# Widening in a convolution and frequency-filter kernel as four float16 products instead of one float32 product

## The reference

```python
x = x + conv3x3(group_norm(x), binary_weight)            # layer 0, sign(w) * alpha
h = einsum('oc,bchw->bohw', w_in, group_norm(x))         # layer 1: 64 -> 256 channels ("widening")
f = rfft2(8x8 patches of h) * fft_filt ; h = irfft2(f)   # a filter per channel and frequency
h = depthwise conv3x3(h, w_dw)
x1, x2 = split(h) ; x = x + einsum('oc,bchw->bohw', w_out, gelu(x1) * x2)
```

## Time and profile before

| | |
|---|---|
| median of three runs | 5607.01 us |
| the profiled execution | 5608.77 us |
| its span (first to last instruction) | 5606.9 us |
| granted TensorE clock, mean | 0.997 of 2.4 GHz |
| TensorE (PE) busy | 5467.3 us, 98% |
| TensorE weight loads (PEld) | 3466.9 us, 62% |
| VectorE (DVE) | 4848.7 us, 86% |
| ScalarE (ACT) | 3314.4 us, 59% |
| GpSimd (POOL) | 3779.9 us, 67% |
| DMA | mean 39 GB/s |

### The profile page before, as it was taken

The page is one execution under the profiler, slowest core; times in us unless marked ns, Lnnn a source line. Parts: engine busy times, 40 slices in busy tenths (PEclk is TensorE's granted clock), DMA queues, the critical chain, the costliest instruction groups (busy, mean ns, idle before and its releaser), DMA issues.

```text
span 5606.9 us, 159317 instructions
## 1 busy us (share of the span) xinstructions
PE 5467.3 (98%) x69156; PEld 3466.9 (62%) x69156; DVE 4848.7 (86%) x6149; ACT 3314.4 (59%) x4194; POOL 3779.9 (67%) x2055
## 2 busy tenths in 40 slices
PE   5999999999999999999999999999999999999998
PEld 4666666666666666666666666666666666666665
DVE  6889888898888989888898888988889888898887
ACT  3656656566565665656656565565655656566565
POOL 3767666676666766666666676666666767676666
PEclk9999999999999999999999999999999999999999
DMA  2011010110101101011010100101011010110000
GB/s 99 18 48 41 35 41 28 51 38 35 51 21 48 38 35 54 18 51 38 35 51 20 55 31 35 54 35 41 31 38 48 35 41 31 48 41 18 22 21 28
DMA packets 43783, 216.61 MB, mean 39 GB/s; under 512 B 5366, under 2 KB 6104, under 8 KB 36952
## 3 DMA queue, kind: packets, MB, share of 16 engines
q1 hardware_dynamic: 43096, 206.42, 9.6%
HBM read 103.64 MB, written 102.76 MB: 37 GB/s over the span
## 4 chain that ended last, share of the span: by engine, by line
PE 78%; DVE 17%; issue 4%; ACT 1%; DMA 0%; DVEq 0%; POOL 0%; SPq 0%; ACTq 0%; POOLq 0%
PE PS L895 19%; PE PS L912 18%; PE PS L857 14%; PE PS L885 14%; DVE v L632 8%; PE PS L925 7%; PE PS L875 4%; DVE g L655 3%; PE PS L866 2%; DVE hf L625 2%; DVE bn L563 1%; DVE PS L648 1%; ACT carry L464 1%; DVE nbx L580 0%; DVE Xa L662 0%
## 5 line engine op out<-in xcount | busy, mean ns | idle before, releaser
L346 POOL TENSOR_TENSOR v_lo<-v,v_hi 128x1024 f16<-128x1024 f32 (+1 forms) x1792 | 3356.8, 1895 | 1712.1 <-ACT v_hi L443 1701.6
L632 DVE TENSOR_TENSOR v<-PS,smul 128x1024 f32<-128x1024 f32 (+1 forms) x1792 | 1903.5, 1084 | 313.4 <-PE PS L895 288.6
L443 ACT ACTIVATE v_hi<-v 128x1024 f16<-128x1024 f32 (+1 forms) x1792 | 1652.5, 945 | 788.8 <-DVE v L632 583.3
L895 PE MATMUL PS<-hf,c_nodes 64*128 64x512 f32 (+1 forms) x7168 | 1724.0, 573 | 55.8 <-DVE v L632 35.5
L912 PEld LDWEIGHTS PS<-c_ext,v_hi 128*128 128x128 f16 x14336 | 1130.4, 97 | 458.1 <-issue 249.5
L912 PE MATMUL PS<-c_ext,v_hi 128*128 128x100 f16 (+2 forms) x14336 | 1257.8, 203 | 20.2 <-ACT carry L464 16.1
L912 PE MATMUL PS<-c_ext,v_lo 128*128 128x100 f16 (+2 forms) x14336 | 1249.8, 202 | 0.0
L912 PEld LDWEIGHTS PS<-c_ext,v_lo 128*128 128x128 f16 x14336 | 1117.9, 97 | 1.4
L625 DVE TENSOR_TENSOR hf<-PS,mult 128x1024 f32<-128x1024 f32 (+1 forms) x896 | 962.9, 1086 | 148.0 <-PE PS L885 134.4
L895 PEld LDWEIGHTS PS<-hf,c_nodes 64*128 64x128 f32 x7168 | 577.0, 185 | 634.6 <-DVE v L632 313.7
L885 PE MATMUL PS<-win_sb,xf 64*128 64x256 f32 x6272 | 850.1, 399 | 4.1 <-ACT xf L432 1.0
(11 more groups left out here) (63 smaller groups left out, 3801.7 us busy)
## 6 DMA issues: line engine op xcount, KB each, us to landing
out_x<-Xa SPq DMA_DIRECT2D x96, 448.0 KB, 2.5
out_x<-Xb SPq DMA_DIRECT2D x96, 448.0 KB, 2.5
Xa<-in_x SPq DMA_DIRECT2D x8, 2240.0 KB, 7.9
Xb<-in_x SPq DMA_DIRECT2D x8, 2240.0 KB, 8.0
Xa<-in_x SPq DMA_DIRECT2D x8, 1792.0 KB, 6.7
Xb<-in_x SPq DMA_DIRECT2D x8, 1792.0 KB, 6.9
Xa<-in_x SPq DMA_DIRECT2D x8, 1344.0 KB, 5.8
Xb<-in_x SPq DMA_DIRECT2D x8, 1344.0 KB, 6.4
```

What stands on the lines that cost most here:

```text
L346: nc.gpsimd.tensor_tensor(v_lo[:, img, :, k0:k1, :], v32[:, V_BUF[kind(b, s)][img][grp], :, 0:k1 - k0, :], v_hi[:, img, :, k0:k1, :], ALU. ...
L443: nc.scalar.activation(v_hi[:, img, :, k0:k1, :], v32[:, V_BUF[kind(b, s)][img][grp], :, 0:k1 - k0, :], ACT.Copy).then_inc(act_vhi[img], 1)
L632: nc.vector.tensor_tensor(v32[:, V_BUF[kind(b, s)][img][grp], :, 0:k1 - k0, :], PS[:, bank:bank + 2, 0:(k1 - k0) * C2].rearrange("p i (k c ...
L895: last = nc.tensor.matmul(PS[:, bank + side, 0:(k1 - k0) * C2], c_nodes[half, :], hf[half, img, k0:k1, :].rearrange("p k c -> p (k c)"), s ...
```

## The change

`w_in` and the spectrum are each held as two float16 parts, high (the rounded value) and low (the rest, rounded), and widening makes four float16 products that accumulate in PSUM: high x high, low x high, high x low, low x low. `win_hi` and `win_lo` are made once by VectorE. The spectrum's high part is made by a second ScalarE pass over `xf` (`spectrum_high`), the low part by GpSimd (`spectrum_low`). `xf` now shares the memory of `xT`, so `pixels` waits for the low part of the strip before. Widening waits for `pool_xl`. Besides, the orders of groups (`HF_ORDER`, `V_ORDER`, `V_BUF`) and the order of instructions of every engine in both kinds of step are new; all waits and banks follow them. Nothing else is changed.

The new order on TensorE: in a conv step projection 0, interpolation (image 0, half 0), widening of groups 3, 2, 0, projection 1, evaluation (0, 2), widening 1, interpolation (0, 1), evaluations (0, 3), (0, 1), (0, 0), then the convolutions and the rest as before. Before it was projection 0, widening 2, 0, interpolation (0, 0), widening 3, 1, evaluation (0, 3), interpolation (0, 1), evaluations (0, 2), (0, 1), projection 1, evaluation (0, 0). In a plain step it is projection 0, interpolation (0, 0), widening 0, 2, interpolation (0, 1), widening 1, evaluation (0, 0), projection 1, widening 3, transposes, evaluations (0, 2), (0, 3), interpolation (1, 0), evaluations (0, 1), (1, 1), interpolation (1, 1), forward transform, evaluations (1, 2), (1, 0), (1, 3). Before it was projection 0, interpolation (0, 0), widening 3, 0, 2, projection 1, widening 1, evaluation (0, 0), interpolation (0, 1), evaluation (0, 2), transposes, interpolation (1, 0), evaluations (0, 3), (0, 1), (1, 1), then the same.

On VectorE filters and weightings follow the same orders; the first carry addition goes ahead of the filters, in a conv step the second residual ahead of weighting (0, 0) and the gate of image 0 behind it, in a plain step the statistics of x are spread anew and the second residual comes behind the gate of image 1. The rest of the diff's core:

```diff
-    HF_ORDER = {"plain": (3, 0, 2, 1), "conv": (2, 0, 3, 1)}
-    V_ORDER = {"plain": ((0, 2, 3, 1), (1, 2, 0, 3)), "conv": ((3, 2, 1, 0), (3, 2, 0, 1))}
+    HF_ORDER = {"plain": (0, 2, 1, 3), "conv": (3, 2, 0, 1)}
+    V_ORDER = {"plain": ((0, 2, 3, 1), (1, 2, 0, 3)), "conv": ((2, 3, 1, 0), (3, 2, 0, 1))}
     V_BUF = {"plain": [{0: 0, 2: 1, 3: 2, 1: 0}, {1: 1, 2: 2, 0: 0, 3: 1}],
- "conv": [{3: 0, 2: 1, 1: 2, 0: 0}, {3: 1, 2: 2, 0: 0, 1: 1}]}
+ "conv": [{2: 0, 3: 1, 1: 2, 0: 0}, {3: 1, 2: 2, 0: 0, 1: 1}]}
...
+        xf = xT
+        xf_hi = sb("xf_hi", [128, NBLK, BPX], F16)
+        xf_lo = sb("xf_lo", [128, NBLK, BPX], F16)
...
+def spectrum_low(n, s):
+    pool.wait_ge(act_xh, n * STRIPS + s + 1)
+    nc.gpsimd.tensor_tensor(xf_lo[:], xf[:], xf_hi[:], ALU.subtract).then_inc(pool_xl, 1)
...
@@ GpSimd, conv and plain order
+            if mid:
+                low_nodes(mid[0], mid[1], 0, 2)
             if more and len(NORM_STEPS.get(t, ())) > 1:
                 low_strip(n + 1, NORM_STEPS[t][1])
             if mid:
                 low_nodes(mid[0], mid[1], 0, 3)
-                low_nodes(mid[0], mid[1], 0, 2)
                 low_nodes(mid[0], mid[1], 0, 1)
                 low_nodes(mid[0], mid[1], 0, 0)
                 low_nodes(mid[0], mid[1], 1, 3)
+            if front:
+                spectrum_low(n, t)
+            if mid:
                 low_nodes(mid[0], mid[1], 1, 2)
                 low_nodes(mid[0], mid[1], 1, 0)
                 low_nodes(mid[0], mid[1], 1, 1)
@@ -375,11 +389,14 @@
                 low_nodes(mid[0], mid[1], 0, 3)
                 low_nodes(mid[0], mid[1], 0, 1)
                 low_nodes(mid[0], mid[1], 1, 1)
+            if front:
+                spectrum_low(n, t)
+            if mid:
                 low_nodes(mid[0], mid[1], 1, 2)
+                low_nodes(mid[0], mid[1], 1, 0)
             if more and len(NORM_STEPS.get(t, ())) > 0:
                 low_strip(n + 1, NORM_STEPS[t][0])
             if mid:
-                low_nodes(mid[0], mid[1], 1, 0)
                 low_nodes(mid[0], mid[1], 1, 3)
...
 def pixels(n, s, bank):
     act.wait_ge(pe_xT, n * STRIPS + s + 1)
+    if n or s:
+        act.wait_ge(pool_xl, n * STRIPS + s)
     nc.scalar.activation(xT[:].rearrange("p k c -> p (k c)"), flat(bank, NBLK * 128), ACT.Copy).then_inc(act_xT, 1)
 def spectrum(n, s, bank):
-    act.wait_ge(pe_xf, n * STRIPS + s + 1)
+    i = n * STRIPS + s
+    act.wait_ge(pe_xf, i + 1)
     nc.scalar.activation(xf[:].rearrange("p k (s f) -> p s k f", f=P * P),
                          PS[:, bank:bank + 2, 0:NBLK * P * P].rearrange("p s (k f) -> p s k f", f=P * P),
                          ACT.Copy).then_inc(act_xf, 1)
+
+def spectrum_high(n, s):
+    i = n * STRIPS + s
+    act.wait_ge(act_xf, i + 1)
+    if i:
+        act.wait_ge(pe_hf, 4 * i)
+    nc.scalar.activation(xf_hi[:], xf[:], ACT.Copy).then_inc(act_xh, 1)
...
@@ ScalarE, conv and plain order
         if more and CONV_FROM <= t <= CONV_TO:
             if up:
                 gelu(up[0], up[1], 0)
+            if more and len(NORM_STEPS.get(t, ())) > 0:
+                strip32(n + 1, 1 - par, NORM_STEPS[t][0], False)
+            if up:
                 keep0(up[0], up[1], 0)
             if more and len(NORM_STEPS.get(t, ())) > 0:
-                strip32(n + 1, 1 - par, NORM_STEPS[t][0], False)
                 strip16(n + 1, 1 - par, NORM_STEPS[t][0], False)
             if more and len(NORM_STEPS.get(t, ())) > 1:
                 strip32(n + 1, 1 - par, NORM_STEPS[t][1], False)
+            if mid:
+                high_nodes(mid[0], mid[1], 0, 2)
+            if more and len(NORM_STEPS.get(t, ())) > 1:
                 strip16(n + 1, 1 - par, NORM_STEPS[t][1], False)
             if mid:
                 high_nodes(mid[0], mid[1], 0, 3)
-                high_nodes(mid[0], mid[1], 0, 2)
             if up:
                 keep1(up[0], up[1], 0)
+            if mid:
+                high_nodes(mid[0], mid[1], 0, 1)
             if front:
                 pixels(n, t, BANK_Q)
-            if mid:
-                high_nodes(mid[0], mid[1], 0, 1)
-                high_nodes(mid[0], mid[1], 0, 0)
+                normalise_patches(n, par, t + 1, True)
             if up:
                 gelu(up[0], up[1], 1)
                 keep0(up[0], up[1], 1)
+            if mid:
+                high_nodes(mid[0], mid[1], 0, 0)
             if front:
                 spectrum(n, t, BANK_P)
+                spectrum_high(n, t)
             if mid:
                 high_nodes(mid[0], mid[1], 1, 3)
             if up:
                 keep1(up[0], up[1], 1)
-            if front:
-                normalise_patches(n, par, t + 1, True)
             if mid:
                 high_nodes(mid[0], mid[1], 1, 2)
                 high_nodes(mid[0], mid[1], 1, 0)
@@ -508,10 +540,10 @@
                 keep0(up[0], up[1], 0)
             if mid:
                 high_nodes(mid[0], mid[1], 0, 0)
-            if up:
-                keep1(up[0], up[1], 0)
             if front:
                 pixels(n, t, BANK_P)
+            if up:
+                keep1(up[0], up[1], 0)
             if mid:
                 high_nodes(mid[0], mid[1], 0, 2)
             if up:
@@ -525,18 +557,18 @@
                 spectrum(n, t, BANK_P)
             if up:
                 keep1(up[0], up[1], 1)
-            if mid:
-                high_nodes(mid[0], mid[1], 1, 2)
-            if more and len(NORM_STEPS.get(t, ())) > 0:
-                strip32(n + 1, 1 - par, NORM_STEPS[t][0], False)
-                strip16(n + 1, 1 - par, NORM_STEPS[t][0], False)
-            if mid:
-                high_nodes(mid[0], mid[1], 1, 0)
             if front:
+                spectrum_high(n, t)
                 if t < STRIPS - 1:
                     normalise_patches(n, par, t + 1, True)
                 elif more:
                     normalise_patches(n + 1, 1 - par, 0, True)
+            if mid:
+                high_nodes(mid[0], mid[1], 1, 2)
+                high_nodes(mid[0], mid[1], 1, 0)
+            if more and len(NORM_STEPS.get(t, ())) > 0:
+                strip32(n + 1, 1 - par, NORM_STEPS[t][0], False)
+                strip16(n + 1, 1 - par, NORM_STEPS[t][0], False)
             if mid:
                 high_nodes(mid[0], mid[1], 1, 3)
...
@@ VectorE, prologue
+nc.vector.tensor_copy(win_hi[:], win_sb).then_inc(dve_prep, 1)
+dve.wait_ge(dve_prep, 3)
+nc.vector.tensor_tensor(win_lo[:], win_sb, win_hi[:], ALU.subtract).then_inc(dve_prep, 1)
...
 def widened(b, s, grp, bank):
     k0, k1 = GROUPS[grp]
-    pe.wait_ge(act_xf, b * STRIPS + s + 1)
+    pe.wait_ge(pool_xl, b * STRIPS + s + 1)
     for k in range(k0, k1):
-        for r in range(IMGS):
-            last = nc.tensor.matmul(PS[:, bank + r, (k - k0) * C2:(k - k0 + 1) * C2], xf[r * C:(r + 1) * C, k, :],
-                                    win_sb[r * C:(r + 1) * C, :], start=True, stop=True)
+        for part, (xf, win) in enumerate(((xf_hi, win_hi), (xf_lo, win_hi), (xf_hi, win_lo), (xf_lo, win_lo))):
+            for r in range(IMGS):
+                last = nc.tensor.matmul(PS[:, bank + r, (k - k0) * C2:(k - k0 + 1) * C2],
+                                        xf[r * C:(r + 1) * C, k, :], win[r * C:(r + 1) * C, :],
+                                        start=part == 0, stop=part == 3)
     last.then_inc(pe_hf, 1)
```

More of the change, by code:

```diff
@@ L701, in image @@
                             weighted(b, s, 0, 1, BANK_Q)
-                        if up:
-                            gated(up[0], up[1], 0)
+                        if done:
+                            residual(done[0], (par + done[2]) % 2, done[1], 1)
                         if mid:
@@ L710, in image @@
                             convolved(n + 1, 1 - par, conv_strips(t)[1], BANK_P)
-                        if done:
-                            residual(done[0], (par + done[2]) % 2, done[1], 1)
                         if up:
@@ L719, in image @@
                             stats_1(n + 1, 1 - par, conv_strips(t)[1])
-                        if more and t == GROUP1_STEP - 1:
-                            channels_1(n + 1)
                         if mid:
@@ L731, in image @@
                             weighted(b, s, 1, 1, BANK_Q)
+                        if more and t == GROUP1_STEP - 1:
+                            channels_1(n + 1)
                     else:
@@ L737, in image @@
                         if mid:
-                            filtered(b, s, 3, BANK_P)
+                            filtered(b, s, 0, BANK_Q)
+                            filtered(b, s, 2, BANK_P)
+                        if more and len(STAT_STEPS.get(t, ())) > 1:
+                            stats_x(n + 1, 1 - par, STAT_STEPS[t][1])
                         if more and t == GROUP1_STEP:
@@ L762, in image @@
                             weighted(b, s, 0, 2, BANK_Q)
-                        if more and len(STAT_STEPS.get(t, ())) > 1:
```

(31 more changed lines are left out.)

122 lines of the change are left out of this document (51 added, 71 removed).

## The result

| | before | after |
|---|---|---|
| median of 4 runs, us | 5607.29 (5606.2 to 5607.81) | 5566.68 (5564.79 to 5567.16) |
| profiled execution, us | 5608.8 | 5564.8 |
| its span, us | 5606.9 | 5563.0 |

The ratio is 0.9927 [0.991, 0.9944]: 40.6 us or 0.73% faster. The forecast was 5509, 98 us faster. The sign is right and the time lies in the range, but less than half of the gain came.

The account below looks back on a forecast made before the run. PE alone was taken to bound convolution steps; in plain steps VectorE was only 1.2 us behind. 105 x 0.48 = 50.4 plus 119 x 0.42 = 50.0 less 0.7 gave 99.7 us: 5608.8 to 5509, range 5450 to 5578.

Parts of the forecast that it names:

- the best stretch, 0.97 us for two blocks, has 0.06 us a block over that: Float32 widening on PE: the best stretch exceeds the 0.427 us streaming of a product pair by 0.06 us a block.
- the convolution step's 0.48: Widening in each of 105 convolution steps: 3.79 to 3.31 us, 0.48 saved, 50.4 us in all.
- about 0.1 us at a group whose bank is released late: PE's widening stretches: the rest of 3.53 and 3.79 us is about 0.1 us at each late-released bank.
- The plain step's 0.42: Each of 119 plain steps: a walk of the new order gave 0.55 us less, minus 0.13 for tighter feed; 50.0 us.
- Rival D: Handoffs between PE and VectorE through the two bank pairs eat everything, so the time stays the same; chance 0.05.
- so all of it counts: Convolution step: it is PE-bound, so the whole 0.48 us saved in widening shortens the step.
- rival A: VectorE, busy 20.09 of 21.27 us, is the wall in plain steps; only convolution steps give, 5558 us; chance 0.12.
- Rival B: The new GpSimd subtraction before widening comes late, from 0.75 us of lateness on a loss; about 5700 us; chance 0.08.
- Rival C: Loads of a row half don't go under its own matmul: 0.204 us a pair, 6080 us; chance 0.05.
- Rival E: The new orders also take out waits that were there: 0.8 us saved a step, 5430 us; chance 0.05.
- The costs of ScalarE and GpSimd: 224 second passes on ScalarE, 0.94 us each, 211 us; 224 subtractions on GpSimd, 1837 ns each, 411 us; both have room.
- The start-up: The prologue: two copies of 128x256 and a wait on VectorE, 0.7 us once.

Follow-up runs that it names:

- e7: Kernel after with VectorE's filtering and weighting over half of the 256 columns, the rest of their outputs zero, PE's work whole; 5408.62 us, 0.9646 to before.
- e9: Kernel before with the new orders, float32 widening and no feed, VectorE's filtering and weighting over half of the columns; 5432.49 us, 0.9689 to before.
- e11: Kernel after with only the product form undone: widening is float32 again, while orders, second ScalarE pass, GpSimd subtraction and waits stay; 5596.32 us, 0.9982 to before.
- e8: Kernel before with VectorE's filtering and weighting over half of the columns, the rest of their outputs zero; 5432.65 us, 0.9689 to before.
- e1: Kernel before with the new orders alone: widening stays one float32 product, no second ScalarE pass, subtraction or their waits; 5583.27 us, 0.9957 to before.
- e2: Kernel before, in its old orders, with the four float16 products, second ScalarE pass and GpSimd subtraction; 5652.46 us, 1.0081 to before.
- e4: Kernel before with the one-column variances and shifts on VectorE reading one SBUF tensor input instead of two; 5590.92 us, 0.9971 to before.
- e3: Kernel after with the one-column variances and shifts on VectorE reading one SBUF tensor input instead of two; 5545.18 us, 0.9891 to before.
- e6: Kernel after without the low x low product and with one-column variances and shifts reading one SBUF tensor input; 5477.21 us, 0.9768 to before.

## Why the prediction was right in sign and too large

- **The step that failed** is "the best stretch, 0.97 us for two blocks, has 0.06 us a block over that" with what followed from it, "only what lies between the products can go". The excess is real, 0.97 - 2 x 0.427 = 0.12 us, but it does not lie between products. It stands once at a group's start (0.32 us instead of 0.2157 to the second product), and again in part at the switch to another operation, which float16 pays too. The trace of before would have shown it: inside a group its pairs of records start 0.216 us apart too. With VectorE short the float32 stretch is 3.32 us in a convolution step and the float16 one 3.26 (e7: 0.45, 0.87, 0.97 and 0.97), and plain steps differ by 0.20 (0 to 4 in the mean, e9 and e7). In place (e11 to after) the form gives 0.17 in a convolution step, where a float32 group whose bank comes late pays more, and 0.12 in the mean of the plain ones: 105 x 0.17 + 119 x 0.12 = 32 us, as the spans have it, and 29.6 by the medians. The sum had 50.4 + 50.0.
- **The term that was mis-sized most** is the convolution step's 0.48. It is the difference of a measured stretch with waits for banks in it (3.79) and a built one nearly without (3.31). The prediction put such waits at "about 0.1 us at a group whose bank is released late"; they were 0.46 over the two stretches (3.79 - 3.33, e8). The stretch goes 3.79, 3.52 (e1, e11), 3.34 (after), the step 27.62, 27.57, 27.40. The orders took 0.27 from the stretch, and the same 0.27 stands again as PE's wait before the convolution; only the form's 0.18 arrives.
- **The plain step's 0.42** rested on a walk of the new order. Measured: 0.20 in step 3, 0.23 to 0.25 in steps 0, 1 and 4, nothing in step 2. The stretch was forecast as 3.16; the sum of its pieces (1.85 to the interpolation, 0.88, 0.54) is 3.27. The prediction counted islands of float16, as many in both orders, but not the widening's own stretches, of which the new plain order has one more. Up to widening's last block PE is 0.15 us earlier than in e1; from there to the transposes it takes 0.93 us, in e1 0.85, where e7 and e9 need 0.54 and 0.63: the transposes wait for VectorE's weighting, and 0.08 is left in the step.
- **Rival D** (handoffs between PE and VectorE eat the gain) had 0.05 and was in part what happened: of the 0.45 us that the convolution stretch became shorter, 0.27 came back as a wait for VectorE. The argument that PE is busy 27.55 of 27.60 us and "so all of it counts" was wrong as it stood: e7's convolution step is 26.77 with the same PE work, 0.63 us below, though PE counts as busy for 27.13 of the 27.39. The records of PE's matmuls overlap, so short delays between their starts don't show as idle time. The case against **rival A** stands: VectorE is no wall of its own in plain steps (0.9 us idle in 21.08), yet it is on the path: with its filters and weightings halved these steps take 20.5.
- **Rival B** (late feed) did not occur, 5.1 us of waits in all; in the old orders it did (e2). **Rival C** (exposed loads) did not either: pairs at 0.109 us with 94 ns loads to the same rows of the array. The Trainium skill (TensorE: Matmul & The Clock Gate, What overlaps and what doesn't) says loads overlap only where the row group differs; this trace disagrees.
- **Rival E** (the orders take out old waits) was given 0.05 and is true in part: 24 us, 21 of them in step 5. Of the 1.40 us of step 5, 1.04 hang on VectorE instructions of one column that the prediction never looked at (e4); the costliest group of them is 26.2 us of 5607. The same thing gave back 10 of those us in step 13, with the feed. Steps 5 and 13 together brought 14 us (24 less 10), where the prediction's 0.42 a plain step had 12.6 for them. That is close, but from another cause, and so luck.
- The costs of ScalarE and GpSimd were right, 951 ns a pass (forecast 0.94) and 1900 ns a subtraction (1837). The start-up, put at 0.7 us, became 4.7 us longer: 2.3 with the orders, 3.4 with the feed, less 1.0 with the form.

What stays open: why the new orders cost 0.11 us in step 2 and 0.33 in step 6 (e1), of which the form gave back 0.10 and 0.18, and why a float32 group with a late bank pays 0.1 us more than a float16 one.

## What to carry to other kernels

A saving that is the difference of a measured stretch and a built one takes the stretch's waits for savings: compare the same form of stretch in both, and get the cost per item from stretches of different lengths, so that a group's start and its items part. Where two engines hand banks back and forth, a PE at 97% busy does not mean that what PE saves arrives; here 30 of 49 us did (e11 to after, PE busy 5434.4 and 5385.8). And sort the groups of a trace by mean time over size too: one instruction of a single column cost 1.28 us a pair (step 13, after to e3), where the whole change gained 3.0.

## What the runs showed of the hardware

A VectorE instruction of one column with two tensor inputs in SBUF waits while GpSimd runs a subtraction on SBUF, and ends with it. Means over 16, in the kernel before:

```profile
L580 DVE SCALAR_TENSOR_TENSOR nbx<-groupx,rstdx 128x1 f32<-128x1 f32 x16 | 26.2, 1636 | 0.7 <-POOL rstdx L330 0.7
L573 DVE SCALAR_TENSOR_TENSOR varx<-groupx 128x1 f32<-128x1 f32 x16 | 13.5, 844 | 0.6
L591 DVE SCALAR_TENSOR_TENSOR var<-group 128x1 f32<-128x1 f32 x16 | 9.2, 576 | 0.6
```

In the kernel after, whose orders place them elsewhere beside GpSimd's work, 1636 ns became 690, 844 became 243, and 576 became 2042 (the groups of after are shown with the result). In the pairs behind the first each of these long ones ends 0.01 to 0.02 us after a GpSimd subtraction. With one input in PSUM, or the second as the scalar of a tensor_scalar, e3 has

```profile
L622 DVE SCALAR_TENSOR_TENSOR var<-PS,group 128x1 f32<-128x1 f32 x16 | 3.5, 219 | 0.6
L612 DVE TENSOR_SCALAR nbx<-groupx,rstdx 128x1 f32<-128x1 f32 x16 | 3.3, 204 | 0.7 <-POOL rstdx L336 0.7
```

which was worth 16 us before, 21.5 after (19.1 by the spans) and 27.7 in e6. The Trainium skill (SBUF — State Buffer, Who interferes with whom) has the rule: VectorE and GpSimd share a pair of SBUF ports under an exclusive lock. The trace agrees, and shows that it holds for an instruction of a single column.

The other surprise is that a float32 product of 64 x 128 with 256 columns streams as fast as its four float16 parts, 0.2157 us for a pair of records against 0.218 for two float16 pairs. Splitting it by hand gains only at the start of a group, unless a part is left out.
